# Forward transforms in four 64x64 tiles of the TensorE array, in an FFT-mixing kernel

## What is computed

```python
m  = mean(x, over all tokens);  f = x - m
ff = (1 - EPS) * f @ f.T / (n - 1) + EPS * eye(64)
y  = (inv(cholesky(ff)) @ f) * gamma + beta                 # layer 0

h  = layer_norm(y, n1_g, n1_b)
xf = rfft2(h, axes=(H, W), norm='ortho')                    # 56 x 29
o1 = relu(complex blockwise product of xf with w1, + b1)    # 8 blocks of 8 channels
o2 = softshrink(complex blockwise product of o1 with w2, + b2)
h  = irfft2(o2) + h + y
z  = layer_norm(h, n2_g, n2_b)
out = gelu(z @ mw1 + mb1) @ mw2 + mb2 + h                   # 64 -> 256 -> 64
```

## Time and profile before

| | before |
|---|---|
| median of three runs | 840.85 us |
| the profiled execution's own time | 842.9 us |
| its span | 841.1 us |
| PE busy with matmuls | 778.3 us (93%) |
| DVE busy | 569.4 us (68%) |
| ACT busy | 378.4 us (45%) |
| POOL busy | 251.9 us (30%) |

### The profile page before, as it was taken

The page is one execution under the profiler, slowest core; times in us unless marked ns, Lnnn a source line. Parts: engine busy times, 40 slices in busy tenths (PEclk is TensorE's granted clock), DMA queues, the critical chain, the costliest instruction groups (busy, mean ns, idle before and its releaser), DMA issues.

```text
span 841.1 us, 17115 instructions
## 1 busy us (share of the span) xinstructions
PE 778.3 (93%) x6823; PEld 542.9 (65%) x6823; DVE 569.4 (68%) x1860; ACT 378.4 (45%) x687; POOL 251.9 (30%) x107
## 2 busy tenths in 40 slices
PE   7999996986799999999999999999999998989987
PEld 5985555875477667666766667676757664746433
DVE  4567777279577767776776777677867695843551
ACT  0011005623164735563556455545554545455455
POOL 4000000932903270427042604360435045413000
PEclk9895557899699999999999999999999999999999
DMA  9943002002000121002100300030001001001012
GB/s 263 276 113 107 1 0 75 3 2 78 1 1 13 34 65 46 24 23 82 29 25 23 95 17 24 23 108 4 23 23 34 2 24 34 23 2 34 23 34 67
DMA packets 10369, 39.41 MB, mean 47 GB/s; under 512 B 1282, under 2 KB 1410, under 8 KB 8834
## 3 DMA queue, kind: packets, MB, share of 16 engines
q1 hardware_dynamic: 10290, 38.31, 15.8%
HBM read 25.46 MB, written 12.85 MB: 46 GB/s over the span
## 4 chain that ended last, share of the span: by engine, by line
PE 80%; DVE 15%; issue 3%; ACT 1%; DMA 0%; DVEq 0%; ACTq 0%
PE psum L1069 11%; PE psum L1078 10%; PE psum L982 7%; PE psum L1047 6%; PE psum L992 6%; PE psum L1023 6%; PE psum L1034 6%; PE psum L1007 6%; PE psum L966 5%; PE psum L829 4%; PE psum L886 4%; DVE stats L588 3%; PE psum L1087 3%; PE psum L953 2%; PE psum L1060 2%
## 5 line engine op out<-in xcount | busy, mean ns | idle before, releaser
L1271 ACT ACTIVATE hid<-psum,hbias 128x448 f32<-128x448 f32 x224 | 124.0, 636 | 80.6 <-PE psum L1069 80.6
L436 POOL TENSOR_TENSOR p_y<-layer,clamped 128x512 f32<-128x512 f32 x64 | 75.5, 1180 | 240.1 <-DVE clamped L698 240.1
L1069 PE MATMUL psum<-n2T,mw1s 64*128 64x448 f32 x448 | 102.7, 577 | 1.7 <-ACT n2T L1264 1.7
L1078 PE MATMUL psum<-hid,prm 128*64 128x448 f32 x448 | 96.3, 552 | 2.0 <-DVE oslice L707 2.0
L401 POOL TENSOR_TENSOR hbuf<-hbuf,prm 112x3584 f32<-112x3584 f32 x7 | 43.4, 6205 | 111.1 <-DVE hbuf L653 111.1
L1047 PE MATMUL psum<-u_r,cst 58*112 58x448 f32 x256 | 60.4, 592 | 15.5 <-DVE rbuf L720 11.3
L1023 PEld LDWEIGHTS psum<-w2s,o_g 128*64 128x64 f32 x1856 | 60.1, 138 | 15.5 <-issue 8.9
L692 DVE TENSOR_TENSOR layer<-psum,prm 128x512 f32<-128x512 f32 x64 | 40.4, 631 | 41.6 <-PE psum L1023 41.6
L1034 PEld LDWEIGHTS psum<-cst,p_y 128*128 128x128 f32 x512 | 61.2, 192 | 11.2 <-issue 5.6
L1023 PE MATMUL psum<-w2s,o_g 128*64 128x64 f32 x1856 | 66.3, 224 | 2.1 <-DVE layer L692 2.1
L1034 PE MATMUL psum<-cst,p_y 128*128 128x112 f32 x512 | 66.7, 277 | 1.2 <-DVE layer L692 1.2
(11 more groups left out here) (130 smaller groups left out, 1308.7 us busy)
## 6 DMA issues: line engine op xcount, KB each, us to landing
xin<-x_dram SPq DMA_DIRECT2D x8, 1568.0 KB, 8.3
out_dram<-oslice SPq DMA_DIRECT2D x56, 224.0 KB, 2.2
ybuf<-x_dram SPq DMA_DIRECT2D x2, 1568.0 KB, 16.8
fbuf<-x_dram SPq DMA_DIRECT2D x2, 1568.0 KB, 19.9
xin<-x_dram SPq DMA_DIRECT2D x4, 392.0 KB, 5.2
n<-x_dram SPq DMA_DIRECT2D x1, 1568.0 KB, 22.1
n<-x_dram SPq DMA_DIRECT2D x4, 392.0 KB, 15.7
prm<-params_dram SPq DMA_DIRECT2D x1, 742.0 KB, 3.9
```

The source lines that it names most:

```text
L436: nc.gpsimd.tensor_tensor(yk, a, b, ALU.subtract).then_inc(y_ready, 1)
L1069: nc.tensor.matmul(t[:, 0:4 * ROWS], mw1s[C * v:C * v + C, HH * m:HH * m + HH], n2T[C * v:C * v + C, s % 2, :], start=True, stop=True).the ...
L1078: last = nc.tensor.matmul(t[C * v:C * v + C, 0:4 * ROWS], pp("mw2")[:, C * m:C * m + C], hid[:, s % 2, m, v, :], start=(m == 0), stop=(m = ...
L1271: nc.scalar.activation(hid[:, s % 2, m, v, :], bank[CH_MLP[i].bank[k]][:, 0:4 * ROWS], ACT.Gelu, bias=hbias[:, m:m + 1]).then_inc(c_act, 1)
```

## The change

`dft_h` and `dft_w` no longer use block diagonal matrices. Each product of 112 x 112 by 112 x 116 becomes four of 56 x 56 (or 56 x 64) by 56 x 58, one for each pair of a row half and a column half of the array: rows 0 to 55 and 64 to 119, output columns 0 and 64 on. For that the two images lie at partitions 0 and 64 instead of 0 and 56 from the whitening on (`RP` = 128), and `h` is read at every second value, so that one product takes one of two neighbouring channels. The two row halves write to different banks.

```diff
 dft_h:
-                    for k in range(8):
-                        t = free_b(i, S1 + k)
-                        for j in range(4):
-                            last = nc.tensor.matmul(t[0:ROWS, j * 2 * KR:(j + 1) * 2 * KR], h_w[:, 4 * k + j, :],
-                                                    cc("f1", ROWS), start=True, stop=True)
+                    for k in range(0, 8, 2):
+                        t = [free_b(i, S1 + k + b) for b in range(2)]
+                        for j in range(8):
+                            for b in range(2):
+                                for h in range(2):
+                                    one = nc.tensor.matmul(t[b][C * h:C * h + H, j * KR:(j + 1) * KR],
+                                                           h_w[C * b:C * b + H, 4 * k + j, h, :], cc("f1")[C * b:C * b + H, :],
+                                                           start=True, stop=True)
 dft_w:
+                        for j in range(n):
+                            at = (4 * k + j) * 128
+                            for h in range(2):
+                                for b in range(2):
+                                    one = nc.tensor.matmul(t[h][C * b:C * b + C, j * KR:(j + 1) * KR],
+                                                           u_r[C * h:C * h + H, at + C * b:at + C * b + C], cc("f2")[C * h:C * h + H, :],
+                                                           start=True, stop=True)
```

Moved and rearranged:

```diff
-L1_DVE = (1, 3, 5, 7)
+L1_DVE = (3, 5, 7)

 DVE, ln2:
-                    for k in range(2):
-                        multiply_rstd(i, k)
+                    multiply_rstd(i, 0)
 DVE, slice 0 of the step:
+                    def second_half():
+                        if behind:
+                            multiply_rstd(i - 1, 1)
+                        next_(ln1_stats, [0])

 PE, dft_h:
-                        if i > 1 and k == 2:
-                            mlp_out(i - 2, SLICES - 1)
-                        if i > 1 and k == 4:
+                        if i > 1 and k == 2:
                             turn_out(i - 2, SLICES - 1)
 PE, end of the step:
                     inv_h(i, 3)
                     if behind:
-                        turn_out(i - 1, 5 if ahead else 6)
+                        mlp_out(i - 1, 6)
+                        turn_out(i - 1, 5)

 SP:
+                for p in range(PAIRS):
                     for s in range(SLICES):
+                        if s == 4 and p + 4 < PAIRS:
+                            sp.wait_ge(pe_a, (p + 3) * A_CHUNKS + 7)
+                            load(p + 4)
                         store(p, s)
```

More of the change, by code:

```diff
@@ L131, in mlp_bank @@
         return {"n2": BANK_X, "mlp": (BANK_M, 2)[what[1] % 2], "out": 1}[what[0]]
-    return BANK_X if i == PAIRS - 2 and what == ("out", SLICES - 2) else BANK_M
+    return BANK_X if what == ("out", SLICES - 2) else BANK_M
 class MlpChunks:
@@ L201, in build @@
         xin = sb("xin", [ROWS, FREE])
-        ybuf = sb("ybuf", [ROWS, FREE])
-        hbuf = sb("hbuf", [ROWS, WP * CW])
-        rbuf = sb("rbuf", [ROWS, WP * CW])
-        fbuf = sb("fbuf", [ROWS, FREE])
-        n2 = sb("n2", [ROWS, FREE])
-        xT = sb("xT", [128, WP * ROWS])
+        ybuf = sb("ybuf", [RP, FREE])
+        hbuf = sb("hbuf", [RP, WP * CW])
+        rbuf = sb("rbuf", [RP, WP * CW])
+        fbuf = sb("fbuf", [RP, FREE])
+        n2 = sb("n2", [RP, FREE])
+        xT = sb("xT", [128, WP * RP])
         u_r = sb("u_r", [128, CH * 2 * KR])
@@ L798, in first_h @@
                     y4 = ybuf[:].rearrange("p (w j h) -> p w j h", j=CH, h=2)
-                    mean, rstd = (small[:, j, early].unsqueeze(2).unsqueeze(2).broadcast_to((ROWS, Y0_DVE, CH, 2)) for j in (0, 3))
+                    mean, rstd = (small[:, j, early].unsqueeze(2).unsqueeze(2).broadcast_to((RP, Y0_DVE, CH, 2)) for j in (0, 3))
                     nc.vector.tensor_tensor(h_tok[:, early], y4[:, early], mean, ALU.subtract).then_inc(h0_sub, 1)
@@ L1046, in inv_h @@
                             rows = slice(C * d, C * d + KR)
-                            one = nc.tensor.matmul(t[d][0:ROWS, 0:7 * C], cc("invh")[rows, ROWS * m:ROWS * m + ROWS], g[rows],
+                            one = nc.tensor.matmul(t[d][:, 0:7 * C], cc("invh")[rows, RP * m:RP * m + RP], g[rows],
                                                    start=(m == 0), stop=(m == 1))
@@ L1160, in step @@
                         mlp_out(i - 1, 5)
-                    if not ahead:
-                        turn_out(i - 1, 5)
-                        mlp_out(i - 1, 6)
                     inv_h(i, 3)
                     if behind:
-                        turn_out(i - 1, 5 if ahead else 6)
+                        mlp_out(i - 1, 6)
+                        turn_out(i - 1, 5)
                 def last_mlp(i):
+                    turn_out(i - 1, SLICES - 1)
                     transpose_n(i, 0)
@@ L1353, in _ @@
                     act.wait_ge(pe_a, 7 + k + 1)
-                    nc.scalar.copy(ybuf[:, k * 512:(k + 1) * 512], bank[FIRST_WHITEN[k]][0:ROWS, :]).then_inc(whitened, 1)
+                    nc.scalar.copy(ybuf[:, k * 512:(k + 1) * 512], bank[FIRST_WHITEN[k]]).then_inc(whitened, 1)
                 ev_x(1, range(7))
```

191 lines of the change are left out of this document (97 added, 94 removed).

## The result

The changed kernel takes **855.9 us** (median of four runs, 852.5 to 857.1) where the kernel before takes 841.4 on the same chip: by the means of the runs 1.015 times as long, 95% interval 1.010 to 1.021. The profiled execution has 852.5 us and a span of 850.6, which is 9.5 more than the span before.

What follows compares the result with a forecast made beforehand. PE was taken to bound the kernel, with DVE the one to watch. Gains 21.6 + 6.0 + 5.3, less 0.1 and 4.8, made 28.0 us off 842.9, or 814.9; adjusted to the median, the forecast was 813, range 798 to 843.

Steps and rivals of the forecast that it cites:

- The transforms on PE: dft_h and dft_w: with four tiles at once they take 6.7 us a step instead of 12.8, 6.1 less.
- Who is last: Between dft_h and layer_1: DVE's chain sets the start of layer_1, at 483.8 instead of 488.11.
- From layer_1 on: layer_1 to transpose_n: 4.3 us gained, 0.7 given back each step; net 3.6 in steps 1 to 6, 21.6 together.
- The first step: First step, without MLP: layer_1 starts at about 159.2 instead of 165.22, 6.0 us gained.
- The last step: Last step, no whitening to wait for: dft_h to the first transpose of n2 gets shorter, net 5.3 us gained.
- The start: Start of the program: the clearing there, together with the doubled stores, costs 0.1 us.
- The clock: PE's new wait between dft_w and whiten: clock falls in two of five of seven steps, costing 4.8 us.
- not more than two tiles at a time: Rival in dft_h and dft_w: eight matmuls need over 200 ns; 848 to 857 us, likeliest 850; chance of slower 0.16.
- The floor under each start: Rival in both transforms: each matmul with its load costs PE's queue some 26 ns; no change, 841 us; chance 0.05.

Runs made afterwards that it cites:

- e12: Kernel before with the rearrangements, four layer_1 chunks on DVE, dft_h in column halves, dft_w in four tiles, whiten's first chunk emptied earlier, e1's wait; 831.7 us.
- e6: Changed kernel with e1's wait, mlp_out back inside dft_h, four layer_1 chunks on DVE and ACT's new wait moved to PE; 837.6 us.
- e3: Changed kernel with every second product of dft_h and dft_w left out; 839.8 us in a single run.
- e5: e4 with four instead of three chunks of layer_1 on DVE; 835.8 us, 0.993 of before.
- e7: e6 with dft_w again as 29 block diagonal products of 120 x 128 by 120 x 116; 842.3 us.
- e4: Kernel before with only the change's rearrangements (order, three layer_1 chunks on DVE, loads), transforms as they were; 839.8 us, 0.998 of before.
- e1: Changed kernel with one added wait: POOL begins the first residual only after DVE's six masked weight products; 841.7 us, 1.000 of before.

## Why the prediction was wrong

**The transforms on PE: the burst right, the sum wrong.** "32 groups x 2 x 52 = 3.3 us, and 29 x 2 x 58 = 3.4 us" priced 488 matmuls at the pace of a group. That pace was measured at 55 ns a group, as forecast, and the question that the prediction put (are four at once possible?) has the answer it gave. But it took the pace of a short burst for the whole. Step 4 took 11.4 us instead of 6.7. Of the 4.7 more, 2.5 are PE's idle time marked issue, about 1.0 is the lower clock behind it (184 matmuls of `dft_w` take 4.02 us where 187 take 3.00 in e12), and about 1.1 is a pace of 16 ns a matmul over whole transforms instead of 13.7 (in e6's step 3, at the full clock, the two keep PE for 7.8 us without their gaps). This is the step that failed: the change multiplied the instructions of the two transforms by four, and their supply, 27 to 29 ns a matmul with its load, was no term of the sum. The prediction does have the words "the mean distance between two starts never goes under 29 ns", but that is the 59 ns of a pair in `layer_2`, which its 64 columns account for. That the supply has the same size is a coincidence as far as the runs show, and it could not be read from rows 4.

**Who is last.** "`layer_1` starts at 483.8" is 11.0 us behind a `dft_h` that has the 1.7 us of `mlp_out` ahead of it; 14.6 was measured, since PE itself was late. Behind supply DVE does stand, as said: e3 shows the wait for `ybuf`, and DVE's instruction at 487.75, 9.6 us behind `dft_h`, where 9.3 was forecast. But even there `layer_1` doesn't start sooner than 12.4 us behind `dft_h`, since the clock falls at that wait in each of the steps 3 to 6.

**From layer_1 on.** "`transpose_n` follows at 491.2": 7.4 us behind `layer_1`'s start; it was 8.16. With three chunks on DVE ACT is last. e5 prices that at 4 us for the run. The wider columns and the changes of tile shape were in the sum with 0.7 us a step. Against e5, e7 shows 1.1: 0.3 for `turn_out`, which the sum had at nothing, and 0.4 each for `whiten` and the transposes. The rearrangement as it stood was worth 1.3 us in the run (e4). In steps 1 to 6 together a gain of 21.6 was forecast, a loss of 2.1 was measured.

**The first step**: 6.0 gained was forecast, 7.3 lost was measured. The prediction knew that DVE and POOL exclude each other, saw POOL at 148.54, and didn't ask what DVE does at that moment: six operations, of which the first starts 0.23 us ahead of POOL's. Before, none of the six waited; in the change three of them did. With the wait of e1 the forecast is half right: 73.2 instead of 76.3. **The last step** gained 1.8, not 5.3, for the same supply and an ACT that was last; e4, with the old transforms, gains 2.7 there. **The start**: 0.1 was forecast, 1.9 measured; of the added waits only the data they protect was read, not that a table load stands behind one. Its part is at most the 1.58 us that PE waits for the copy behind it. The rest isn't shown: kernels without the moved load start their first `dft_h` anywhere from 147.6 (e4) to 150.8 (e12).

**The clock**: 4.8 us were forecast from waits for DVE, by a fall in two of five steps. It does fall, behind idle time marked issue: for 3.4 us in each of four of the steps 1 to 6, where it never fell before, and for 3.4 us more than before in the last. At 1.0 us a fall, as in step 4, that is about 5 us. The size fits, the cause was another.

**The rivals.** The slower one ("not more than two tiles at a time", 850 us) has the sign and nearly the time, by luck: its mechanism is refuted, eight matmuls take 110 ns. The floor under each start is refuted too as it was put, starts lie 13.7 ns apart on average; yet a floor of that size, in the supply of instructions and not in PE, is what happened. The Trainium skill's figure (TensorE: Matmul & The Clock Gate, "Wait — 56ns, not 53.3ns?") of about 25 ns between starts does not hold for four tiles, by the 64 matmuls at 481.80.

## What to carry to other kernels

Before a kernel is split into smaller matmuls, count instructions as a resource of their own: where PE can do the 127 matmuls with their loads of one packet in less than about 3.5 us, it waits for the next. Put work that takes long per instruction inside the burst, not ahead of it or behind. And look for long and short instructions on DVE and POOL that start together: which comes first differed here between two layouts with the same starts, and an explicit wait makes the good order certain.
